# A cross-attention kernel whose head loads in finer transfers and multiplies its first key block in another order

## What is computed

```python
def heads(x, W, b, S):
    return (x @ W.T + b).reshape(B, S, NH, HD).transpose(0, 2, 1, 3)   # NH = 16, HD = 32
q, k, v = heads(query, Wq, bq, Sq), heads(key, Wk, bk, Sk), heads(value, Wv, bv, Sk)
q_prime = relu(einsum('bhnd,fd->bhnf', q, Wqf))                        # f = 64
k_prime = relu(einsum('bhnd,fd->bhnf', k, Wkf)) * attention_mask[:, None, :, None]
kv = einsum('bhnf,bhne->bhfe', k_prime, v)
out = einsum('bhmf,bhfe->bhme', q_prime, kv) / (q_prime . sum(k_prime) + 1e-08)
x = x + (out @ Wo.T + bo)          # query = layernorm(x), key = value = ctx_2048, 12544 rows
x = x + gated_layer(layernorm(x))
x = x + experts(layernorm(x))
```

## Time and profile before

| what | us |
|---|---|
| median of 3 runs | 894.99 |
| lowest and highest of them | 892.92 and 896.53 |
| the profiled execution, its own time | 893.13 |
| its span, first to last instruction | 891.3 |
| PE busy in it | 878.6 (99%) |
| DVE, ACT and POOL busy | 618.5, 509.4 and 366.0 |

### The profile page before, as it was taken

The page is one execution under the profiler, slowest core; times in us unless marked ns, Lnnn a source line. Parts: engine busy times, 40 slices in busy tenths (PEclk is TensorE's granted clock), DMA queues, the critical chain, the costliest instruction groups (busy, mean ns, idle before and its releaser), DMA issues.

```text
span 891.3 us, 14331 instructions
## 1 busy us (share of the span) xinstructions
PE 878.6 (99%) x4596; PEld 728.0 (82%) x4596; DVE 618.5 (69%) x1000; ACT 509.4 (57%) x917; POOL 366.0 (41%) x210
## 2 busy tenths in 40 slices
PE   8999999999999999999999999999999999899998
PEld 6888888888888888888888888888888898447566
DVE  5777777777777777777777777777777786522422
ACT  5566666666666666666666666666666664100000
POOL 4444444444444444444444544444454331000000
PEclk9999999999999999999999999999999999999999
DMA  6222121212110101010101010101010002946500
GB/s 239 90 76 73 70 70 71 74 67 74 44 47 24 47 24 47 24 47 24 47 24 47 24 47 24 47 24 47 24 48 24 0 2 99 442 174 277 214 1 13
DMA packets 12552, 64.13 MB, mean 72 GB/s; under 512 B 1905, under 2 KB 2673, under 8 KB 11377
## 3 DMA queue, kind: packets, MB, share of 16 engines
q1 hardware_dynamic: 11808, 63.58, 19.1%
q10 hardware_dynamic: 720, 0.25, 0.1%
HBM read 63.56 MB, written 0.26 MB: 72 GB/s over the span
## 4 chain that ended last, share of the span: by engine, by line
PE 95%; DVE 2%; DMA 2%; issue 1%; SPq 0%; ACT 0%; POOL 0%; DVEq 0%; ACTq 0%; POOLq 0%
PE kv_ps L648 10%; PE f_ps L635 10%; PE v_bank L553 10%; PE v_bank L554 10%; PE k_bank L553 10%; PE k_bank L554 10%; PE v_bank L555 10%; PE k_bank L555 10%; PE kv_ps L824 5%; PE v_bank L719 3%; PE k_bank L719 2%; PE kv_ps L719 2%; DMA x_sb<-in_x 1%; PE f_ps L710 1%; PE v_bank L656 1%
## 5 line engine op out<-in xcount | busy, mean ns | idle before, releaser
L336 POOL TENSOR_TENSOR ksum_acc<-ksum_acc,kf 128x1024 f32<-128x1024 f32 x96 | 230.9, 2405 | 188.6 <-DVE kf L923 188.6
L428 ACT ACTIVATE fb<-f_ps 128x256 f32<-128x256 f32 x392 | 149.5, 382 | 174.5 <-PE f_ps L635 168.2
L916 DVE TENSOR_TENSOR kf<-f_ps,fb 128x256 f32<-128x256 f32 x392 | 165.6, 423 | 109.0 <-ACT fb L428 103.5
L329 POOL TENSOR_TENSOR ctx_lo<-ctx_raw,ctx_hi 128x512 fp32r<-128x512 f32 x94 | 123.2, 1311 | 178.2 <-ACT ctx_hi L403 178.2
L635 PEld LDWEIGHTS f_ps<-bd,keys 128*128 128x128 f32 x784 | 146.3, 188 | 33.6 <-issue 1.3
L635 PE MATMUL f_ps<-bd,keys 128*128 128x256 f32 x784 | 155.9, 281 | 1.1 <-DVE kf L916 1.1
L553 PE MATMUL v_bank<-wv_hi,ctx_lo 128*128 128x512 f32 x388 | 153.2, 395 | 0.0
L554 PE MATMUL v_bank<-wv_lo,ctx_hi 128*128 128x512 f32 x388 | 152.6, 393 | 0.0
L553 PE MATMUL k_bank<-ctx_hi,wk_lo 128*128 128x512 f32 (+1 forms) x392 | 152.4, 389 | 0.0
L554 PE MATMUL k_bank<-ctx_lo,wk_hi 128*128 128x512 f32 (+1 forms) x392 | 152.2, 388 | 0.0
L555 PE MATMUL v_bank<-wv_hi,ctx_hi 128*128 128x512 f32 x388 | 151.0, 389 | 0.0
(11 more groups left out here) (190 smaller groups left out, 813.5 us busy)
## 6 DMA issues: line engine op xcount, KB each, us to landing
ctx_raw<-in_ctx SPq DMA_DIRECT2D x48, 512.0 KB, 3.2
early<-in_early SPq DMA_DIRECT2D x14, 512.0 KB, 4.3
swi_b<-in_swib SPq DMA_DIRECT2D x1, 4096.0 KB, 14.2
w_out<-in_wout SPq DMA_DIRECT2D x1, 4096.0 KB, 24.8
fc<-in_fc SPq DMA_DIRECT2D x1, 4096.0 KB, 34.1
early<-in_proj SPq DMA_DIRECT2D x1, 4096.0 KB, 12.2
swi_b<-in_fc SPq DMA_DIRECT2D x1, 4096.0 KB, 13.4
w_out<-in_proj SPq DMA_DIRECT2D x1, 4096.0 KB, 12.4
```

Source lines behind the costliest of these rows:

```text
L329: pool.tensor_tensor(ctx_lo[:, s, :, cols], ctx_raw[:, :, t % 2 * P:(t % 2 + 1) * P], ctx_hi[:, s, :, cols].bitcast(f32), ALU.subtract).th ...
L336: pool.tensor_tensor(ksum_acc[:, :].rearrange("p (j f) -> p j f", f=P), ksum_acc[:, :].rearrange("p (j f) -> p j f", f=P), kf[:, t % 2, :, ...
L428: act.activation(fb[:, i % 2, :, :], f_ps[i % 2][:, :].rearrange("p (j x f) -> p j x f", j=2, x=2) [:, :, 1, :], ACT.Copy).then_inc(fb_rea ...
L916: dve.tensor_tensor(kf[:, t % 2, 2 * i:2 * i + 2, :], f_ps[i % 2][:, :].rearrange("p (j x f) -> p j x f", j=2, x=2)[:, :, 0, :], fb[:, i % ...
```

## The change

It touches the head alone; the loop and everything behind it keep their instructions.

1. **Transfers.** `wk` comes in three pieces (m = 0, m = 1, m = 2 and 3) and context half 0 in two (two of its four column groups each). The order is wk piece 0, half 0 in two pieces, wk pieces 1 and 2, `x`, half 1, `ident`, `wv`, `wq`.
2. **Splits.** ACT and DVE cut by these pieces. POOL has no share of the first chunk's low parts any more; DVE makes them all. DVE computes the moments of `x` before the low parts of half 1, and the normalized rows behind them.
3. **Key products.** `keys_0` runs all four m for half 0 first, then all four for half 1, with the transposes behind the first of these. Its waits are by piece.
4. **Fillers.** Three in place of six.
5. **Fourth half.** Half 3 goes into `ctx_raw_b`, and its load waits for the low parts of half 1, not for those of half 2.
6. **ACT's order behind that.** `wv` is cut behind the keys of m = 0, both tiles of half 2 behind the keys of m = 1, both of half 3 behind the keys of m = 3; before, one tile stood behind each. DVE and POOL cut `wv` correspondingly later.

```diff
         def _(sp):
+            load_wk(0)
             for b in range(2):
-                sp.dma_start(wk_raw[:, ms, :, :], wk_in[:, ms, :, :]).then_inc(wk_loaded[b], 16)
-                if b == 0:
-                    sp.dma_start(ctx_raw[:, :, :], ctx_in[0, :, :, :]).then_inc(ctx_loaded, 16)
-                    sp.dma_start(ctx_raw_b, ctx_in[1, :, :, :]).then_inc(ctxb_loaded, 16)
+                ks = ctx0_parts[b][1]
+                sp.dma_start(ctx_raw[:, ks, :], ctx_in[0, :, ks, :]).then_inc(ctxa_loaded[b], 16)
+            load_wk(1)
+            load_wk(2)
+            sp.dma_start(x_sb[:, :], x_in).then_inc(x_loaded, 16)
+            sp.dma_start(ctx_raw_b, ctx_in[1, :, :, :]).then_inc(ctxb_loaded, 16)
+            sp.dma_start(ident[:, :], ident_in).then_inc(ident_loaded, 16)
             sp.dma_start(wv_raw, wv_in).then_inc(wv_loaded, 16)
-            sp.dma_start(x_sb[:, :], x_in).then_inc(x_loaded, 16)
-            sp.dma_start(ident[:, :], ident_in).then_inc(ident_loaded, 16)
             sp.dma_start(wq, wq_in).then_inc(wq_loaded, 16)
...
             sp.wait_ge(ctx0_lo_ready, 2)
-            load_half(2)
-            load_half(3)
+            sp.dma_start(ctx_raw[:, :, :], ctx_in[2, :, :, :]).then_inc(ctx_loaded, 16)
+            sp.wait_ge(ctx0_lo_ready, 4)
+            sp.dma_start(ctx_raw_b, ctx_in[3, :, :, :]).then_inc(ctx3_loaded, 16)
...
         def _(pool):
-            for b in range(2):
-
-                pool.wait_ge(ctx_hi_ready, b + 1)
-                cols = slice(b * HALF, (b + 1) * HALF)
-                pool.tensor_tensor(ctx_lo[:, 0, KC - 1, cols], (ctx_raw, ctx_raw_b)[b][:, KC - 1, :],
-                                   ctx_hi[:, 0, KC - 1, cols].bitcast(f32), ALU.subtract).then_inc(ctx_lo_ready, 1)
...
         def _(act):
             for m in range(KC):
                 keys_high(0, 0, m, k_first[m], CHUNK)
-                split_ctx_high(2 + m // 2, 1, m)
+                if m == 0:
+                    act.wait_ge(wv_loaded, 16)
+                    act.activation(wv_hi[:, :, :], wv_raw, ACT.Copy).then_inc(wv_hi_ready, 1)
+                if m == 1:
+                    act.wait_ge(ctx_loaded, 16)
+                    for t in (0, 1):
+                        split_tile_high(1, t)
+            act.wait_ge(ctx3_loaded, 16)
+            for t in (2, 3):
+                split_tile_high(1, t, ctx_raw_b)
...
         def _(pe):
             pe.wait_ge(consts_set, 3)
-            keep_warm(6, ksum_acc[:, 0:P], ksum_acc[:, 0:D])
-            pe.wait_ge(wk_lo_ready, 1)
-            for b in range(2):
-                pe.wait_ge(ctx0_lo_ready, b + 1)
-                pe.wait_ge(ctx_lo_ready, b + 1)
-                keys_0(0, b)
-                keys_0(1, b)
-            pe.wait_ge(wk_lo_ready, 2)
-            for m in (2, 3):
-                for b in range(2):
-                    keys_0(m, b)
-                if m == 2:
+            keep_warm(3, ksum_acc[:, 0:P], ksum_acc[:, 0:D])
+            for m in range(KC):
+                if m < 3:
+                    pe.wait_ge(wk_lo_ready, m + 1)
+                keys_0(m, 0, m == 0)
+            for m in range(KC):
+                keys_0(m, 1, m == 0)
+                if m == 0:
                     pe.wait_ge(ident_loaded, 16)
                     pe.wait_ge(z0_ready, 2)
                     transposes(f_ps[0], z0).then_inc(z0T_done, 1)
```

More of the change, by code:

```diff
@@ L160, in perceiver_kernel @@
         ident_loaded = sem("ident_loaded")
-        wk_loaded = [sem("wk_loaded0"), sem("wk_loaded1")]
+        wk_loaded = [sem(f"wk_loaded{i}") for i in range(3)]
+        ctxa_loaded = [sem("ctxa_loaded0"), sem("ctxa_loaded1")]
         bdk_loaded = sem("bdk_loaded")
@@ L199, in perceiver_kernel @@
         ctx_lo_ready = sem("ctx_lo_ready")
+        ctx3_loaded = sem("ctx3_loaded")
+        ctx0_hi_ready = sem("ctx0_hi_ready")
         ctx0_lo_ready = sem("ctx0_lo_ready")
@@ L401, in split_ctx_high, with split_tile_high @@
             def split_ctx_high(h, s, t):
-                act.wait_ge(ctx_loaded, 16 * h)
-                act.activation(ctx_hi[:, s, :, t * P:(t + 1) * P], ctx_raw[:, :, t % 2 * P:(t % 2 + 1) * P], ACT.Copy)\
+                act.wait_ge(ctx_loaded, 16 * (h - 2))
+                split_tile_high(s, t)
+            def split_tile_high(s, t, raw=ctx_raw):
+                act.activation(ctx_hi[:, s, :, t * P:(t + 1) * P], raw[:, :, t % 2 * P:(t % 2 + 1) * P], ACT.Copy)\
                    .then_inc(ctx_hi_ready, 1)
@@ L470, in period, with split_wk_high, split_ctx0_high @@
                          splits=((2 * c + 4 + t // 2, s, t),) if t < splits else ())
[L472 to L475, removed]
-            split_wk_high(0)
-            act.wait_ge(ctx_loaded, 16)
-            act.activation(ctx_hi[:, 0, :, 0:HALF], ctx_raw[:, :, :], ACT.Copy).then_inc(ctx_hi_ready, 1)
+            def split_wk_high(i):
+                act.wait_ge(wk_loaded[i], 16)
+                act.activation(wk_hi[:, wk_parts[i], :, :], wk_raw[:, wk_parts[i], :, :], ACT.Copy).then_inc(wk_hi_ready, 1)
+            def split_ctx0_high(i):
+                raw, ks, at = ctx0_parts[i]
+                act.activation(ctx_hi[:, 0, ks, at:at + HALF], raw[:, ks, :], ACT.Copy).then_inc(ctx0_hi_ready, 1)
+            split_wk_high(0)
+            for i in range(2):
+                act.wait_ge(ctxa_loaded[i], 16)
+                split_ctx0_high(i)
+            split_wk_high(1)
+            split_wk_high(2)
             act.wait_ge(ctxb_loaded, 16)
-            act.activation(ctx_hi[:, 0, :, HALF:CHUNK], ctx_raw_b, ACT.Copy).then_inc(ctx_hi_ready, 1)
-            split_wk_high(1)
+            split_ctx0_high(2)
+            split_ctx0_high(3)
             act.wait_ge(bdk_loaded, 16)
             act.activation(bd[:, 0, :], bdk, ACT.Copy).then_inc(bd_hi_ready, 1)
-            act.wait_ge(wv_loaded, 16)
-            act.activation(wv_hi[:, :, :], wv_raw, ACT.Copy).then_inc(wv_hi_ready, 1)
             act.wait_ge(bias_loaded, 32)
@@ L555, in three, with keys_0 @@
                 return pe.matmul(out_ps, st_hi, mv_hi, start=False, stop=stop, **kw)
-            def keys_0(m, b):
+            def keys_0(m, b, first=False):
                 cols = slice(b * HALF, (b + 1) * HALF)
                 for k in range(KC):
+                    if first and k % 2 == 0:
+                        pe.wait_ge(ctx0_lo_ready, 2 * b + k // 2 + 1)
                     last = three(k_first[m][:, cols], wk_hi[:, m, k, :], wk_lo[:, m, k, :], ctx_hi[:, 0, k, cols],
@@ L882, in _, with moments_of @@
             halves = [slice(0, D // 2), slice(D // 2, D)]
-            def layer_norm(n, dst, src, ready):
+            def moments_of(src):
                 link(dve.bn_stats(stat[:, 0:6], src))
@@ L888, in layer_norm, with normed @@
                 dve.tensor_scalar(stat[:, 8:9], stat[:, 7:8], LN_EPS, None, ALU.add).then_inc(var_ready, 1)
+            def normed(n, dst, src, ready):
                 dve.wait_ge(rstd_ready, n)
@@ L979, in queries_out, with wk_low, ctx0_low @@
                                       0.0, None, ALU.max).then_inc(qf_ready, 1)
[L981 to L991, removed]
+            def wk_low(i):
+                dve.wait_ge(wk_hi_ready, i + 1)
+                dve.tensor_tensor(wk_lo[:, wk_parts[i], :, :], wk_raw[:, wk_parts[i], :, :],
+                                  wk_hi[:, wk_parts[i], :, :].bitcast(f32), ALU.subtract).then_inc(wk_lo_ready, 1)
+            def ctx0_low(i):
+                raw, ks, at = ctx0_parts[i]
+                dve.wait_ge(ctx0_hi_ready, i + 1)
+                dve.tensor_tensor(ctx_lo[:, 0, ks, at:at + HALF], raw[:, ks, :],
+                                  ctx_hi[:, 0, ks, at:at + HALF].bitcast(f32), ALU.subtract).then_inc(ctx0_lo_ready, 1)
             wk_low(0)
@@ L996, in _ @@
             wk_low(1)
+            wk_low(2)
+            dve.wait_ge(x_loaded, 16)
+            moments_of(x_sb[:, :])
+            ctx0_low(2)
+            ctx0_low(3)
+            normed(1, z0, x_sb[:, :], z0_ready)
             dve.wait_ge(bd_hi_ready, 1)
@@ L999, in _ @@
                .then_inc(bd_lo_ready, 1)
-            dve.wait_ge(x_loaded, 16)
-            layer_norm(1, z0, x_sb[:, :], z0_ready)
+            dve.wait_ge(bias_loaded, 32)
+            keys_low(0, 0, 0, k_first[0], CHUNK)
+            dve.wait_ge(z0T_done, 1)
+            dve.tensor_copy(z0_T, f_ps[0][:, :].rearrange("p (k t) -> p k t", k=KC)).then_inc(z0T_ready, 1)
             dve.wait_ge(wv_hi_ready, 1)
@@ L1004, in _ @@
                               wv_hi[:, 0:KC // 2, :].bitcast(f32), ALU.subtract).then_inc(wv_lo_ready, 1)
[L1005 to L1010, removed]
+            for m in (1, 2):
+                keys_low(0, 0, m, k_first[m], CHUNK)
             dve.wait_ge(q_done, 1)
```

18 lines of the change are left out of this document (11 added, 7 removed).

## The result

The changed kernel takes 891.6 us in the median of 11 runs (890.17 to 893.58), the kernel before 893.39 in the median of 11 (892.84 to 896.53). The ratio is 0.997, with a 95% interval of 0.9957 to 0.9982: faster by 0.3%, or 2.7 us, and so inside the 0.5% that the prediction counts as no change. The two medians alone are only 1.8 apart; the lowest times are 2.7 apart. The forecast was 891.5, from a gain of 3.2.

What follows compares the result with a forecast made beforehand. TensorE was taken to bound the kernel, so head gains count one for one: -2.6 + 1.6 - 0.7 - 1.55 is -3.2 us, taking the median 894.99 to 891.8, set at 891.5; range 888.5 to 894.3 (8 in 10).

Steps and rivals of the forecast that it cites:

- The bound: Whole kernel: TensorE is busy 878.6 of 891.3 us, so what PE gains in the head comes out one for one.
- Part 1: Head, start of the key matmuls: at 6.2 instead of 8.79, straight behind the fillers, a gain of 2.6 us.
- Part 2: Head, before block 2's keys: PE waits for the last key weights from 9.1 to 10.7, a loss of 1.6 us.
- Part 3: Head, before the transposes and before the queries: the holes of 0.7 and 1.55 us both go.
- Part 4: Later work, costed at nothing: `wv` cuts and second chunk's low tiles stay covered, POOL ending at 27.4, 1.2 us early.
- Sum: Start of the queries: 19.9 instead of 23.09, a gain of 3.2 us, with bounds 2.5 to 3.8.
- the first rival: Head transfers: each further one adds 0.6 us, block 2 starts at 12.5, PE gains only 1.4, ending at 893.5; 8%.
- A cost of each further transfer: Same as the first rival: three more transfers make the last key weights 1.8 us later; 893.5, chance 8%.
- A falling clock: Head, behind the new hole or at the start: PE runs matmuls at twice the time, 1.6 us lost, 893.1; 10%.
- POOL as the last: Second chunk's keys wait for POOL's low tiles: at 5.6 us delay the kernel is 1.2 us slower, 896.2; 6%.

## Why the prediction was right, and where it was not

**The bound: right.** The loop is unchanged and every tenth gained ahead of the queries came out at the end, within 0.2 us over seven profiles at clock 1.000.

**Part 1, start of the keys, -2.6: measured -2.3 to -2.4** (6.45 for 6.2, against 8.79; by the second key matmul 6.57 against 8.98). The fillers were last, as said, but I took the point at which they become fast, 5.19, as fixed; it came one matmul later here, and it moves by up to a microsecond between executions. It was luck that this hardly touched the total: with six fillers 2.1 us of it went and the queries moved by 0.16.

**Part 2, the new hole, 1.6: measured 1.7, but in two places.** The hole before block 2 was 1.0: the low weights were there at 11.09, 0.4 later than said, less the 0.7 that PE already stood before block 1 and the 0.25 of part 1. That second hole I had put at nothing. The failed step is the landing of the piece for m = 1, 6.0 by interpolation and 7.21 in the trace. The interpolation goes by bytes alone and leaves out the time of issue: the piece is issued at 2.13, behind the first of ACT's small loads (1.78), where the same byte was issued at 1.19, ahead of all three. That fits the experiment with late small loads, which brought the piece to 6.31; that the issue time is the whole cause isn't shown.

**Part 3, the old holes, -2.25: right.** Both went, as they did with six fillers and in the coarse form. The normalized rows were done by 13.95 (13.8 said), and 2.81 became 0.74 once POOL was not beside it.

**Part 4, cover: right.** POOL was done at 27.84 (27.4 said) with 1.1 us to spare, and taking the buffer away turned the cover into a wait.

**Sum.** -3.2 said, -2.8 measured in the profiles; the difference is parts 1 and 2. That the median came within 0.1 us of 891.5 is luck. The forecast starts from 894.99, a median of three; with 11 runs the median of before is 893.39, and a gain of 3.2 from there is 890.2. The changed kernel's median in turn is that of a set with six of 11 executions below clock 1.000. What the prediction had right is the path, and a gain 0.4 too large. (Its 893.5 for the first rival should read 893.3 or 893.6, by the base that is taken; nothing rests on it.)

**The rivals.** A cost of each further transfer: the pieces in the middle were late by 0.5 to 1.2, but half 1, which ends 2,304 KB, was usable at 10.81 where 10.7 was interpolated, and moving 241 KB away brought the pieces forward. The coarse version, with two transfers fewer, had its last weights at 8.31 and 9.14, on both sides of 8.77. So no price of 0.6 us for each transfer, though a smaller one, or one of issue time, isn't excluded. The fixed cost of about 2.0 us that the Trainium skill gives (DMA: Bandwidth & Descriptors, Anatomy of one DMA), there for transfers issued from GpSimd, did not add up over these, which SP issues in one queue: ACT could take four pieces within 3.8 us. A falling clock: not behind the holes of this change, but real behind 2.81 us. POOL as the last: no. Of the lock that the Trainium skill describes (SBUF — State Buffer, the two separate sides) the trace has a clear case: DVE's half of `wv` from 19.19, 1.23 us, and POOL's from 19.23, 3.41 instead of the 2.41 of the kernel before. That 2.41 was not alone either: it started 0.07 ahead of DVE's normalization, and there DVE was the one that took longer.

## What to carry to other kernels

An earlier start only counts up to the next wait: here six fillers or three, a difference of 2.1 us at the start, moved the queries by 0.16. Put first the operands that many products can use, let each product wait for its own piece, and look at every other transfer that is in flight meanwhile, those of other queues too; here 241 KB that nobody needed yet delayed the weights by 0.5 to 0.9 us. And before reading a few tenths of a per cent out of medians, sort the executions by granted clock.

## What I had not expected of the hardware

The spread of this kernel's runs is mostly one event. Executions lie at clock 1.000, 0.998 or 0.996, some 1.7 us apart, and in the traces the slow matmuls of the 0.998 ones stand in one place of the tail, where the clock falls to its lower level (0.55 over the 3.8 us shown above). Ahead of it lie some 3 us in which PE had two waits (0.82 and 0.58) and only transposes and the router's narrow products. An equal wait of 0.82 before the same kind of transposes, some 60 us earlier, was followed by full rate in every profile. With 0.86 us of useless products in one of the two waits none of five executions fell. A wait of 2.81 us in the head was followed by 3.3 us at 0.50; waits of 1.29, 1.30 and 1.39 us in the head (three fillers before, four pieces) were followed by matmuls at full rate.
